# Two-layer graph network: dense layers started inside the attention's last rounds, early ELU on GpSimd, and a rebuilt passage from projection to attention

## What is computed

```python
h = relu(layernorm(x));  x = x + smooth(h, adj)           # two products with adj
h = relu(layernorm(x));  x = x + attention_and_mlp(h)
# attention_and_mlp, 8 heads of 64:
Wh  = einsum('nf,hfd->hnd', h, W)
e   = leaky_relu(e_src[:, :, None] + e_dst[:, None, :], 0.2)   # e_src = Wh.a1, e_dst = Wh.a2
att = softmax(where(adj > 0, e, -9e15))
enc = elu(att @ Wh), heads side by side                        # 2048 x 512
out = relu(enc@W1.T+b1) -> 256; relu(@W2.T+b2) -> 128; relu(@W3.T+b3) -> 256; @W4.T+b4 -> 512
```

## Time and profile before

| | us |
|---|---|
| median of 3 runs | 982.78 (980.93 to 983.69) |
| the profiled execution | 983.48 |
| its span, first to last instruction | 981.7 |
| TensorE products busy | 867.9 (88%) |
| VectorE busy | 732.6 (75%) |
| ScalarE busy | 387.2 (39%) |
| GpSimd busy | 315.5 (32%) |

### The profile page before, as it was taken

One profiled execution on the slowest core, in us unless ns is written; L12 is line 12 of the kernel. 1 busy time (PEld: TensorE's weight loads), 2 busy tenths in 40 slices (PEclk: granted clock), 3 DMA queues, 4 the chain that ended last, 5 costly groups with the idle time before them and its releaser, 6 DMA issues. The chain is left out here.

```text
span 981.7 us, 16813 instructions
## 1 busy us (share of the span) xinstructions
PE 867.9 (88%) x5140; PEld 756.0 (77%) x5140; DVE 732.6 (75%) x1208; ACT 387.2 (39%) x698; POOL 315.5 (32%) x295
## 2 busy tenths in 40 slices
PE   1577889997999999989379999999999999948993
PEld 1466668886788888768279999999999999945551
DVE  5999992227555866666798999999999999966761
ACT  2511111211212121235266666666666666624330
POOL 1323343440000000047435555555555534300000
PEclk9799999998999999999779999999999999988998
DMA  9999520004723232040150000000000000012231
GB/s 332 407 312 299 190 86 0 0 0 159 206 87 105 87 106 86 1 170 0 36 199 23 22 21 23 23 21 21 27 27 22 22 21 22 0 54 97 86 129 46
DMA packets 36296, 87.70 MB, mean 89 GB/s; under 512 B 7056, under 2 KB 7952, under 8 KB 36240
## 3 DMA queue, kind: packets, MB, share of 16 engines
q1 hardware_dynamic: 35216, 82.98, 25.1%
q0 software_dynamic: 1040, 4.26, 1.2%
HBM read 74.45 MB, written 12.78 MB: 89 GB/s over the span
## 5 line engine op out<-in xcount | busy, mean ns | idle before, releaser
L930 DVE SCALAR_TENSOR_TENSOR l_q<-bank,l_neg_d,mask 128x512 fp32r<-128x512 f32 x512 | 338.6, 742 | 30.3 <-PE bank L1091 30.3
L1091 PE MATMUL bank<-l_parts,l_q 128*128 128x260 f32 x2048 | 250.8, 284 | 13.5 <-DVE l_q L930 13.5
L1091 PEld LDWEIGHTS bank<-l_parts,l_q 128*128 128x128 f32 x2048 | 248.8, 190 | 13.8 <-issue 11.7
L73 PE MATMUL bank<-l_x_hi,l_s_hi 128*128 128x512 f32 x256 | 102.7, 401 | 49.4 <-DVE l_x_lo L244 48.9
L961 ACT ACTIVATE l_mask<-mask 128x512 fp32r (+1 forms) x256 | 136.5, 619 | 0.7 <-PE bank L1111 0.5
L1111 PE MATMUL bank<-l_parts,l_mask 128*128 128x260 f32 x1024 | 129.6, 287 | 0.0
L1111 PEld LDWEIGHTS bank<-l_parts,l_mask 128*128 128x128 f32 x1024 | 128.1, 191 | 0.0
L73 PE MATMUL bank<-l_g_hi,l_a_hi 128*128 128x512 f32 x256 | 101.1, 395 | 6.2 <-DVE l_a_lo L609 5.9
L593 POOL TENSOR_TENSOR l_prod<-wh,l_a 128x512 f32<-128x512 f32 x32 | 37.5, 1195 | 214.4 <-ACT wh L572 206.7
L74 PE MATMUL bank<-l_x_lo,l_s_hi 128*128 128x512 f32 x256 | 101.1, 395 | 0.0
L75 PE MATMUL bank<-l_x_hi,l_s_lo 128*128 128x512 f32 x256 | 101.0, 394 | 0.0
(11 more groups left out here) (151 smaller groups left out, 1178.8 us busy)
## 6 DMA issues: line engine op xcount, KB each, us to landing
rows<-adj_t SPq DMA_DIRECT2D x48, 512.0 KB, 3.9
l_sum_a<-adj SPq DMA_DIRECT2D x16, 512.0 KB, 6.5
l_rows_b<-adj_t SPq DMA_DIRECT2D x16, 512.0 KB, 7.2
l_sum_b<-adj SPq DMA_DIRECT2D x16, 512.0 KB, 8.7
l_src<-e_rows SPq DMA_DIRECT2D x32, 256.0 KB, 3.1
wh_store<-wh POOLq DMA_DIRECT2D x1, 4160.0 KB, 14.0
l_h<-x SPq DMA_DIRECT2D x4, 1024.0 KB, 13.0
x<-x SPq DMA_DIRECT2D x1, 4096.0 KB, 15.0
```

Of the source, the lines that this page charges most:

```text
L73: pe.matmul(acc, hi, rhs_hi, start=first, stop=False, skip_group_check=True)
L930: v.scalar_tensor_tensor(out=q[:, i, :], in0=bank[S_BANKS[hh]][:], scalar=neg_d[:, i, h:h + 1], in1=mask[:, i, cols], op0=ALU.is_ge, op1=A ...
L1091: return pe.matmul(bank[Q_BANKS[hh][t]][:, 0:PW], q[:, i, t * P:(t + 1) * P], parts[:, pair_slot, hh, i, :], start=i == 0, stop=i == T - 1)
```

## The change

In the projection: the loops are unrolled (`in_turns` for `skewed`). Three of the four groups of score transposes are put inside the loop, at TensorE's steps 8, 12 and 16, with two banks in turn, and VectorE copies them at its steps 9, 13 and 17. For the last two tiles VectorE makes one of the two score products. The source scores of the first round are spread by two products with a selecting matrix straight into the banks. Negated destination scores, the arguments and the exponentials of the factors are made in this block, ahead of its end. The rows are stored in four parts.

In the attention: the first pair's first head is prepared in halves, all on GpSimd, with ScalarE's copies of the high parts, and TensorE may start when the first half is there. VectorE starts with its choices, makes one product and two low parts of the second head between the choices of the first and the second head.

The dense layers are in the attention's block. SyncE issues their weights and the first load of x1 in round 12, behind its load of round 12's source scores. In rounds 13, 14 and 15 VectorE makes the shares of chunks 0, 1 and 2 behind its choices; GpSimd averages them and makes the ELU's parts, ScalarE its exponentials; TensorE transposes chunk 0 among the last q phase. Only the last four tiles have their ELU on VectorE, tile by tile. GpSimd adds the last bias. The first-layer sums of a chunk are made ahead of the second layer of the chunk before, with more banks and buffers. The tiles of the dense layers lie where tiles of the attention have been (`one_place`).

At the end: one conditional on each engine, in the same block, instead of two blocks.

```diff
-def skewed(eng, count, stages, pause=None):
...
+def in_turns(count, *stages):
+    for k in range(count + max(lag for _, lag in stages)):
+        yield k
+        for work, lag in stages:
+            if 0 <= k - lag < count:
+                work(k - lag, (k - lag) % 2)
...
@@ projection, SyncE
-                sp.wait_ge(e_copied, 4)
-                sp.dma_start(e_rows, e_t).then_inc(stored, 16)
+                for q in range(4):
+                    cols = slice(q * 512, (q + 1) * 512)
+                    sp.wait_ge(e_copied, q + 1)
+                    sp.dma_start(e_rows[:, cols], e_t[:, cols]).then_inc(stored, 16)
@@ projection, GpSimd
-                    for n in range(2):
+                    for n in range(2 if t < OWN else 1):
@@ projection, VectorE
+                    else:
+                        v.wait_ge(wh_ready, t + 3)
+                        v.wait_ge(e_ready, 2 * t + 2)
+                        v.tensor_tensor(per_head(prod[:, b, 1, :]), wh[:, t, :, 0:HD], per_head(a_b[:, 1, :]),
+                                        ALU.mult).then_inc(own_prod, 1)
+                        v.wait_ge(own_prod, t - OWN + 1)
+                        reduce_part(t, b, 1)
+                        v.wait_ge(prod_ready, 2 * OWN + t - OWN + 2)
+                        reduce_part(t, b, 0)
...
+                for k in in_turns(T, (cut_turned, 0), (reduce_e, 2)):
+                    if k < G8 // 2:
+                        more_statistics(k, k % 2)
+                    if k == G8 // 2:
+                        second_norms()
+                    if k in (9, 13, 17):
+                        take_e_t((k - 9) // 4)
@@ projection, TensorE
+                for k in in_turns(T, (turn, 0), (project, 1)):
+                    if k in (8, 12, 16):
+                        turn_e(range(k - 8, k - 4))
+                pe.wait_ge(sel_ready, 2)
+                pe.wait_ge(e_copied, 1)
+                for hh in range(2):
+                    pe.matmul(bank[6 + hh][:], sel[:, hh, :], e_t[:, 0:512], start=True, stop=True
+                              ).then_inc(src_spread, 1)
+                turn_e(range(12, T))
@@ attention, SyncE
+                for r in range(1, LAST + 1):
+                    load_src(r)
+                    if r == LAST - 3:
+                        sp.wait_ge(q_done, T + 2 * T * (LAST - 3))
+                        sp.wait_ge(m_done, T + T * (LAST - 3))
+                        for dst, src_w in ((w1_s, w1_t.rearrange("(k p) f -> p k f", p=P)),
+                                           (b1_s, b1), (b2_s, b2), (b3_s, b3),
...
+                            sp.dma_start(dst[:], src_w).then_inc(w_loaded, 16)
...
+                        dense.load(sp, 0, x1_store)
@@ attention, VectorE
+                choose(0, 0, 0, slice(0, QW))
+                v.tensor_tensor(first_whole[3], wh[:, :, 1, :], fac["A"][:, :, 1:2].to_broadcast([P, T, HE]),
+                                ALU.mult).then_inc(second_whole_ready, 1)
...
+                def choose_last(r, k, b):
+                    choose_pair(r, k, b)
+                    c = 2 * k + b - 1
+                    if c >= 0:
+                        v.wait_ge(summed, STEPS * (r + 1))
+                        dense.shares(v, c, 1, fine, retry_chain)
+                last_rounds(choose_last)
+                first_head, second_head = combine(v, LAST, slice(T - GT, T), H // 2 - 1)
+                dense.take_lo(v, 0)
...
@@ attention, ScalarE, in serve
                         take_m_sums(r)
+                        if not more and r == LAST - 3:
+                            a.wait_ge(w_loaded, 16 * 8)
+                            a.activation(w1_hi[:], w1_s[:], ACT.Copy).then_inc(w1_hi_ready, 1)
+                        if not more and r > LAST - 3:
+                            dense.exp_chunk(a, r - (LAST - 2))
+                        if not more and r == LAST:
+                            dense.take_hi(a, 0)
                         if more or r < LAST:
                             take_mask(r + 1, 0, after)
                             take_mask(r + 1, 1, after)
...
+                for c in range(CHUNKS):
+                    if c + 1 < CHUNKS:
+                        dense.relu1(a, c + 1, 0)
+                    dense.relu2(a, c)
+                    if c + 1 < CHUNKS:
+                        dense.relu1(a, c + 1, 1)
+                    for m in range(K3):
+                        dense.relu3(a, c, m)
+                    if c == 0:
+                        for i in range(GT * EARLY, T):
+                            dense.exp_tile(a, i)
+                    if c + 2 < CHUNKS:
+                        dense.take_hi(a, c + 2)
@@ attention, GpSimd
+                first_product(0, 0)
+                first_product(0, 1)
+                first_product(1, 0)
+                first_rest(0, 0)
+                first_rest(0, 1)
...
+                        if not more and r > LAST - 3:
+                            dense.average_chunk(p, r - (LAST - 2))
                         first_head()
+                        if not more and r > LAST - 3:
+                            dense.elu_early(p, r - (LAST - 2))
...
+    def average_chunk(self, p, c):
+        n = self.GT * H // 2
+        p.wait_ge(self.share_ready, 2 * c + 2)
+        for k, z in enumerate(self.halves(c)):
+            share = self.share[:, (2 * c + k) * n:(2 * c + k + 1) * n, :]
+            p.tensor_tensor(z, z, share.to_broadcast([P, n, HD]), ALU.mult).then_inc(self.averaged, 1)
+            p.wait_ge(self.averaged, 2 * c + k + 1)
+            if c:
+                p.wait_ge(self.enc_ready, 2 * c - 1 + k)
+            p.tensor_scalar(self.neg[k], z, 0.0, None, ALU.min).then_inc(self.neg_ready, 1)
+        for k, z in enumerate(self.halves(c)):
+            p.wait_ge(self.neg_ready, 2 * c + k + 1)
+            p.tensor_scalar(z, z, 0.0, -1.0, ALU.max, ALU.add).then_inc(self.pos_ready, 1)
+    def exp_chunk(self, a, c):
+        for k in range(2):
+            a.wait_ge(self.neg_ready, 2 * c + k + 1)
+            a.activation(self.neg[k], self.neg[k], ACT.Exp).then_inc(self.exp_ready, 1)
@@ attention, TensorE
+                def turn_first(i):
+                    if i >= 8:
+                        if i == 8:
+                            pe.wait_ge(m_bank_free, GT * (LAST + 2))
+                        dense.turn(pe, 0, i - 8)
+                def dense_layers(of):
+                    of.sum1(pe, 0, 0)
+                    for k in range(KC):
+                        of.turn(pe, 1, k)
+                    of.sum1(pe, 0, 1)
+                    for c in range(CHUNKS - 1):
+                        of.sum1(pe, c + 1, 0)
+                        of.sum2(pe, c)
+                        of.sum1(pe, c + 1, 1)
...
+                        of.sum3(pe, c)
+                        if c + 2 < CHUNKS:
+                            for k in range(KC):
+                                of.turn(pe, c + 2, k)
+                        for t in range(GT - 1):
+                            of.sum_row(pe, c, t)
+                        if c == CHUNKS - 2:
+                            of.sum2(pe, c + 1)
+                        of.sum_row(pe, c, GT - 1)
```

More of the change, by code:

```diff
@@ L75, in split_product @@
     return pe.matmul(acc, lo, rhs_hi, start=False, stop=True, skip_group_check=True)
-def skewed(eng, count, stages, pause=None):
-    most = max(stage[1] for stage in stages)
-    def turn(k, parity, first, last):
-        for work, lag, *tiles in stages:
-            if first >= lag and last - lag < (tiles[0] if tiles else count):
-                work(k - lag, (parity + lag) % 2)
-    def turns(first, end):
-        pairs = (end - first) // 2
-        with eng.Fori(0, pairs) as j:
-            for b in range(2):
-                turn(2 * j + first + b, (first + b) % 2, first, end - 1)
-        if (end - first) % 2:
-            turn(end - 1, (end - 1) % 2, end - 1, end - 1)
-    for k in range(most):
-        turn(k, k % 2, k, k)
-    if pause:
-        turns(most, pause[0])
-        pause[1]()
-        turns(pause[0], count)
-    elif most < count:
-        turns(most, count)
-    for k in range(count, count + most):
-        turn(k, k % 2, k, k)
 def if_set(eng, flag):
@@ L129, in load_half_rows, with one_place @@
                  ).then_inc(rows_loaded[slot], 16)
+def one_place(nc, ctx, *groups):
+    made = []
+    for k, group in enumerate(groups):
+        with ExitStack() as within:
+            keep = ctx if k == len(groups) - 1 else within
+            made.append([keep.enter_context(nc.sbuf_tensor(name, shape, dt)) for name, shape, dt in group])
+    return made
 def smooth_features(nc, bank, G, rows, rows_loaded, x, adj, adj_t):
@@ new lines, in _ @@
+                sp.wait_ge(q_done, T + 2 * T * (LAST + 1))
+                dense.load(sp, 1, x1_store)
+                for c in range(CHUNKS):
+                    dense.store(sp, c, out)
+                    if c + 2 < CHUNKS:
+                        dense.load(sp, c + 2, x1_store)
```

(39 more changed lines are left out.)

1038 lines of the change are left out of this document (551 added, 487 removed).

## The result

| | before | after |
|---|---|---|
| median | 982.04 (980.93 to 984.59, 7 runs) | 988.22 (985.52 to 991.65, 7 runs) |
| span of the profiled execution | 981.7 | 986.3 |
| behind the last VectorE instruction | 12.8 | 4.2 |

The changed kernel takes 1.0056 of the time before, with a 95% interval of 1.004 to 1.0073: slower by about 0.6%, where 970 and a gain were forecast. The profiled execution of the changed kernel took 988.22, so it may stand for the median.

A forecast was written before the change was run, and what follows sets the result against it. TensorE bounds the attention (busy 311.2 of 320 us); behind it TensorE alternates with VectorE and ScalarE. Terms -5.2 + 2.5 + 8.5 + 3.2 - 13.9 - 8.2 = -13.1 gave 970.4 profiled, 969.7 median, predicted 970; range 956 to 979.

The forecast's parts named there:

- the price of GpSimd's minimum and maximum: Early ELU in the attention's last rounds: each one-input GpSimd operation on half a chunk was taken as 1.1 us.
- the sign of being wrong: Early ELU: wrong if GpSimd's one-input operation is not near 1.1 us, or TensorE shows no gap in rounds 13 and 14.
- Rival C: Last three attention rounds: GpSimd alone bounds them, slower than before from 2.6 us an operation, 996 at 4.0; chance 0.05.
- ELU in the attention: Rounds 13 and 14: ScalarE's exponentials wait for GpSimd and delay the copy TensorE needs; +7.5 and +1 us.
- GpSimd just keeps up: Rounds 13 and 14: GpSimd finishes averages, heads and sums in time, at 840.6 us.
- rival B: Early ELU: GpSimd's one-input operations cost what two-input ones do, 1.96 us; about 6 more, 976; chance 0.13.
- Last phase: End of the attention: chunk 0's transposes among the last products wait for ScalarE and VectorE; +3.2 us.
- dense layers: Behind the attention: all ELU work and the bias addition off VectorE, 97.9 us down to 84; -13.9 us.
- 6.4 at chunk 2: Dense layers: wait at chunk 2's transposes, behind ScalarE's exponentials and VectorE's ELU of the last four tiles; 6.4 us.
- SyncE's queue: Round 12: source scores of round 13 stand behind weight loads, delaying ScalarE's fill and masks; +2.5 us.
- Passage: From projection to attention: first attention product at 489.2, round 0's second phase ending at 510.2; -5.2 us.
- Behind the last instruction: End of the span: one conditional left, reached by TensorE before the last addition, 4.6 us left of 12.8; -8.2 us.

The follow-up runs named there:

- e3: Changed kernel with GpSimd's ELU minimum and maximum replaced by two-input instructions, leaving those steps out of the computation; 970.76 against 982.71 before, ratio 0.9883.
- e6: Changed kernel with VectorE combining the last round's first head ahead of chunk 0's low parts instead of behind; 985.07 against 982.43 before, ratio 1.0029.
- e5: Changed kernel with TensorE waiting for both halves of the first head's parts before the attention's first product; 990.90 against 982.43 before, ratio 1.0099.
- e1: Changed kernel with SyncE issuing dense weights and first x1 load behind round 13's source scores, not ahead; 983.90 against 982.71 before, ratio 1.0015.
- e2: Changed kernel with ScalarE's exponentials of chunks 0 and 1 moved to the end of rounds 13 and 14; 985.68 against 982.71 before, ratio 1.0039.
- e7: Changed kernel with the early ELU's one-input passes on ScalarE and the -1 put into the splits; 960.83 against 982.43 before, ratio 0.9777.
- e4: Kernel before, without its two skipped conditional blocks at the end; 972.17 against 982.71, ratio 0.9901.

## Why the prediction was wrong

**The step that failed** is the price of GpSimd's minimum and maximum. It was taken as 1.1, bounded by ScalarE's 1.06 and by GpSimd's own two-input 1.96. The row nearest in engine was named as the upper end without a reason that one input can't cost more than two. It does: 2.78 and 3.62 against 1.91. So the upper end was wrong, and GpSimd's round, worked out as 23.9, was 32.3. The prediction had named this price itself as the sign of being wrong. The trace of before showed no such operation at this size, so the upper end should have stayed open until some row excluded it. What the Trainium skill states pointed the same way: "GPSIMD Engine Reference", Engine selection, gives one input as roughly line rate and warns only of two, and in this trace the one-input form is the slower of the two (2.7 ns a column against 1.9); the measurement decides.

**Rival C was the case.** Its own working, ten times the excess over 1.1 less 2.4 of slack, gives with the measured prices (excess 1.68 twice and 2.52 twice, mean 2.1) 18.6, so 989.0 for 988.2 measured. The closeness is partly luck: the rounds and the last phase came out 14.9 above forecast, not 18.6, and the other terms together 2.8 above it. But that it decides from 2.6 an operation was right, and 5% was too little for a price that no row showed. "No row of GpSimd at 1040 columns is above 2.33" was true and was no argument, as all those rows have two inputs.

**ELU in the attention, +8.5, was +18.0.** The mechanism (ScalarE waits for the minimum, TensorE for ScalarE's copy) is there in both rounds. Missing was that GpSimd's round of 32.3 bounds from then on: "GpSimd just keeps up" rested on four operations of 1.1. e3 takes 9.3 of the 18.0 out: from round 13's mask phase to round 15's it has 55.1, where the changed kernel has 64.4 and the kernel before 46.4 (809.12 to 855.52). That leaves 8.7 at a price of 1.9. The forecast had 8.5 for a price of 1.1, and rival B some 6 more in all for 1.96; so the rest of the forecast's chain was charged too dearly. And e3's -12.0 is close to the forecast's -13.1, though its operations cost 1.9: had the price come out so, the forecast would have been met partly by luck.

**Last phase, +3.2, was +8.6, and dense layers, -13.9, were -8.4.** The first is in the main the same price once more (at 1.9, in e3, that wait is 2.38): the minimum of chunk 2 ends at 885.3, ScalarE's exponential and high part behind it, VectorE's low part at 886.95, and TensorE had waited 5.12. Of the 5.5 missing in the second, 5.1 are chunk 1's wait of 6.72 in place of 1.6. That VectorE's first head would run beside GpSimd's long instructions there wasn't worked out, though the earlier trace rows had shown a 0.2 us instruction held for 2.02 and the passage was costed by it; e6 shows what it costs and which GpSimd instructions do it. The forecast of 6.4 at chunk 2 was right: 5.95.

**SyncE's queue, +2.5, was +4.9.** The place and the chain were right (fill, eight masks, last quarter of the phase). The step that was off is the time to landing, taken as 3.1 from the earlier trace rows and measured as 8.9 behind the bulk loads; their issues took 4.4 instead of 6.9, which gave 2.5 of it back. ScalarE's fill waited 5.25, where 2.1 to 3.6 were forecast; it cost both the last quarters of the phase, 2.94 and 1.32, and clock.

**Passage, -5.2, was -10.1.** More than half of the surplus is not the passage's. The projection's last product was to end at 474.4, and ended at 471.7 in this trace; before it was 473.2. From there to round 0's second head the forecast had 35.8, and it was 33.6, against 42.2 before. So the passage itself gave 8.6, 2.2 more than forecast. GpSimd's first product started at 479.93 and its parts were ready at 485.36: 5.4 for the five operations against a forecast of 5.8. The forecast let VectorE's and GpSimd's products run one behind the other and had ScalarE late for the next phase by 2.5; that wait was 0.74. (Also, TensorE doesn't end all its transposes at 474.5 in the kernel before, as the prediction says: the last four of sixteen run at 479.19.)

In the nine traces of changed kernels the projection's last product ends anywhere from 471.7 to 476.6, while the way from there to the second head is 33.4 to 33.7 in all but e5. In the four traces where it ends last (e1, e2, e6, e7) the granted clock between 420 and 424 was 0.57 to 0.75, in the other five 1.00; that gives some of the spread, and what sets it off is open. A single pair of traces can be off by 5 us in its landmarks for this reason.

**Behind the last instruction, -8.2, was -8.6**: right, and e4 shows the same price from the other side.

## What to carry to other kernels

An operation that no row of the trace shows has no upper bound in a row of another form: if ten of them would turn the sign, that is worth a good part of the chance. Before work is moved to an idle engine, add up that engine's whole round with the work in it; here 23.9 us were worked out for a round of 23.2, which left no room for an error of price. A pass of one input belongs on ScalarE where it has room: the same early ELU with its passes there, and the -1 folded into the splits, took 28 us less. Where a short instruction races a long one on another engine, look at the margin before you trust a median: here less than half a us decided over nearly 5.

## What the runs showed of the hardware

- GpSimd, 128x1024 fp32: product of two inputs 1.91; minimum or maximum with a constant 2.77; maximum and addition in one instruction 3.62. ScalarE makes a relu of that size in 1.05.
- Beside GpSimd's two-input instructions VectorE's products of 0.43 us took up to 4.49, ending with GpSimd's; beside its one-input instructions most took their usual time (0.42 at 891.87 in the changed kernel; 0.69, 0.43 and one of 1.02 in e6).
- A load of source scores behind some 2.5 MB in the same queue could be used 8.9 us after its issue; the median of such loads was 3.2.
- Two conditional blocks that are skipped cost 10.5 us at the kernel's end, about 5 each.
